# Attention on one core: one ring of three PSUM banks per unit, three banks for pieces, values one slot later

## The chip, the cores and the metric

One core of a Trainium2 chip runs the whole program. TensorE (PE) does matmuls and transposes, VectorE (DVE) and ScalarE (ACT) read its results out of PSUM, GpSimd (POOL) works on SBUF only, SyncE (SP) issues the DMAs. The metric is the device time of one execution in microseconds, lower is better. PSUM has 8 banks of 128 partitions x 512 float32; the program divides them by hand.

## The reference, cut to what matters

Four layers, each as x = x + layernorm(layer(layernorm(x))): a Mamba2 mixer with an MLP, a LoRA MLP, attention, and a linear layer whose weights come from a table. The change touches the third and the fourth, which run interleaved:

```python
def _L1_attn_ref(x, w_qkv, w_o):          # x: 8 batches x 256 tokens x 512
    qkv = x @ w_qkv                        # 32 query heads, 8 key and value heads, 16 wide
    xq, xk = _apply_rope(xq), _apply_rope(xk)
    scores = jnp.einsum('bhsd,bhtd->bhst', xq, keys) * scale
    scores = jnp.where(causal, scores, -jnp.inf)
    probs = jax.nn.softmax(scores, axis=-1)
    out = jnp.einsum('bhst,bhtd->bhsd', probs, values)
    return out @ w_o
```

The kernel keeps float32 accuracy by splitting each operand in a rounded high part and a low part (the difference), and multiplies three times.

## The kernel before, in words

The attention of a batch is cut into 24 **units** (`UNITS`, L1659): for each of the 8 key heads, unit r=0 holds the first 128 queries of its four query heads (they see 128 keys only), and units r=1 and r=2 the last 128 queries of two heads each (256 keys). A unit passes through these steps, each a function of that name:

- `scores(u)` on PE: the products of queries and keys, and one matmul that adds the mask, into a PSUM bank of `S` (two banks, u % 2).
- `maximum(u)` on DVE: the row maxima, negated. `exponentials(u)` on ACT: four or two activations into `p` in SBUF.
- `transposes(u)` on PE: four transposes of `p` into a PSUM bank of `T` (two banks, u % 2).
- `high(u)` on ACT and then `low(u)` on DVE: the turned probabilities as a high and a low part in SBUF (`pT_hi`, `pT_lo`, two buffers each).
- `values(u)` on PE: the product with the values, accumulated over a group of units in the banks `OT`; `values_out` on ACT copies them out.

Beside the units run **pieces** of other work (`JOBS_AT`, L1665, for each of the 24 slots of a batch; `AHEAD`, L1693, for the first batch). On PE a piece is either four transposes (`x`, `a`, `h`: a normalised tile; `q`, `k`: a stack of two-part queries or keys; `back`: attention output) or a half of a projection, six matmuls of 512 columns (`qq`, `o`, `l`), or the whole of `kv`, twelve of 256. Pieces write to the two PSUM banks `X` in turn. `bank_read` makes PE wait, before a piece, until the piece that had the bank before has been read out. Pieces of batch b+1 (its queries and keys) and b-1 (its output projection and the fourth layer) run while the units of batch b do.

The program is a sequence of **slots**. No scheduler works at run time: each engine goes through the slots in its own instruction order, and waits on semaphores. In slot s:

- PE (L2331): `scores(s+1)`, `values(s-2)`, the pieces of slot s, `transposes(s)`.
- ACT (L2056): `drain(s)` (reads out the pieces of slot s-1 that are its own: `x`, `a`, `h`, `q`, `k`, `kv`, `o`), `values_out` in some slots, `high(s-1)`, `exponentials(s+1)`.
- DVE (L2162): `drain(s)` (its own pieces of slot s-1: the rotations after `qq` and `kv`, `back`, `o`, `l`), `maximum(s+1)`, `turned_low(s)` (the low part of a turned tile), `low(s-1)`, then statistics and normalisations of some slots.
- POOL builds the stacks two slots ahead, and does roots and sums.

The waits that matter: `scores(u)` waits for `ex` of unit u-2 (L2209); `transposes(u)` for `ex` of its own unit and `pl` (`low`) of unit u-2 (L2232, L2233); `values(u)` for `pl` of its own unit (L2244). In the text that follows P(n) is the moment at which PE reaches slot n of a batch, that is, at which it issues `scores(n+1)`; n runs from 0 to 23.

Of the kernel before, what the change touches and what calls it, by code (L numbers as in the profile page):

```python
# [1094 lines left out]
def mlps(nc, d, consts, stream, x1_store, w4_store, hT, w0, late, late_2, raw, prod, a_split, lora_unit, bias, tok, old,  # L1095
# [446 lines left out]
    def tensor_program(pe, mixer_program, attention):  # L1542
# [89 lines left out]
        for g, i, j in spots():  # L1632
# [72 lines left out]
def job_tables():  # L1705


    by_slot, ended_by_slot, bank, before, done, turn, stacked, back = {}, {}, {}, {}, {}, {}, {}, {}
    last = [None, None]
    for s in range(FIRST_SLOT, END_SLOT):  # L1710
        by_slot[s], ended_by_slot[s] = [], []
        mine = [(what, part, tile, s // UNITS + rel) for what, part, tile, rel in JOBS_AT[s % UNITS]] if s >= 0 else []
        for what, part, tile, batch in (*AHEAD.get(s, ()), *mine):
            if not 0 <= batch < BATCH:
                continue
            job = name_of(what, part, tile, batch)
            by_slot[s].append((what, part, tile, batch))
            if job not in bank:
                bank[job] = len(bank) % 2
                before[job], last[bank[job]] = last[bank[job]], job  # L1720
            if what not in HALVED or part:
                done[job] = len(done) + 1
                ended_by_slot[s].append((what, part, tile, batch))
                if what in ("x", "a", "h"):
                    turn[what, tile, batch] = len(turn)
                elif what in ("q", "k"):
                    stacked[job] = len(stacked) + 1
                elif what == "back":
                    back[part, tile, batch] = len(back)
    return by_slot, ended_by_slot, bank, before, done, turn, stacked, back  # L1730
# [26 lines left out]
def attention_layer(nc, d, consts, stream, w_hi, w_lo, l_hi, l_lo, bias, keep, xf, yl, small, buffers, ps, mlp):  # L1757
# [223 lines left out]
    def scalar_program(act):  # L1981
# [58 lines left out]
        def high(u):  # L2040
            act.wait_ge(tr, u + 1)
            wait(act, pv, u - 1)
            act.activation(pT_hi[:, u % 2, :], ps[:, T + u % 2, :], ACT.Copy).then_inc(ph, 1)  # L2043

        def exponentials(u):
            act.wait_ge(mx, u + 1)
            wait(act, tr, u - 1)
            heads, width = (4, P) if u % 3 == 0 else (2, SEQ)
            for h in range(heads):
                last = act.activation(p[:, u % 2, h * width:(h + 1) * width],  # L2050
                                      ps[:, S + u % 2, h * width:(h + 1) * width], ACT.Exp, bias=nmax[:, u % 3, h:h + 1])
            last.then_inc(ex, 1)
# [3 lines left out]
        for s in range(FIRST_SLOT, END_SLOT):  # L2056
            b, n = s // UNITS, s % UNITS
            drain(s)
            if n in (0, 2) and in_batch(b - 1):
                values_out(2, n // 2, b - 1)  # L2060
            if n in (9, 11) and in_batch(b):
                values_out(0, n // 2 - 4, b)
            if n in (18, 20) and in_batch(b):
                values_out(1, n // 2 - 9, b)
            if 0 <= s - 1 < SLOTS:
                high(s - 1)
            if 0 <= s + 1 < SLOTS:
                exponentials(s + 1)

    def vector_program(dve, last_sums, end_stats, scale_sum):  # L2070
# [72 lines left out]
        def maximum(u):  # L2143
            heads = 4 if u % 3 == 0 else 2
            dve.wait_ge(sc, u + 1)
            wait(dve, ex, u - 2)
            dve.tensor_reduce(nmax[:, u % 3, 0:heads], ps[:, S + u % 2, :].rearrange("p (h t) -> p h t", h=heads),  # L2147
                              AX, ALU.max, negate=True).then_inc(mx, 1)

        def low(u):  # L2150
            dve.wait_ge(ph, u + 1)
            wait(dve, pv, u - 1)
            dve.tensor_tensor(pT_lo[:, u % 2, :], ps[:, T + u % 2, :], f(pT_hi[:, u % 2, :]), ALU.subtract).then_inc(pl, 1)  # L2153

# [51 lines left out]
    def tensor_program(pe, first, end):  # L2206
        def scores(u):
            b, g, r = u // UNITS, u % UNITS // 3, u % 3
            wait(pe, ex, u - 1)  # L2209
            if u == 0:  # L2210
                pe.wait_ge(setup, 13)
            if u % UNITS == 0:
                pe.wait_ge(st_out, max(STACKED["q", 0, 1, b], STACKED["k", 0, 1, b]))
            elif u % 6 == 0:
                pe.wait_ge(st_out, STACKED["q", g // 2, 1, b])
                if g == 4:
                    pe.wait_ge(st_out, STACKED["k", 1, 1, b])
            bank = ps[:, S + u % 2, :]
            if r == 0:
# [11 lines left out]
        def transposes(u):  # L2231
            pe.wait_ge(ex, u + 1)  # L2232
            wait(pe, pl, u - 1)  # L2233
            if u == 0:
                pe.wait_ge(mlp["summed"], TPB * NG * NB)
            for k in range(4):
                mm = pe.transpose(ps[:, T + u % 2, k * P:(k + 1) * P], p[:, u % 2, k * P:(k + 1) * P], ident)  # L2237
            mm.then_inc(tr, 1)

        def values(u):  # L2240
# [10 lines left out]
            if r == 0:  # L2251
                pe.matmul(ps[:, OT, :], v(0), pT_hi[:, u % 2, :], start=fresh, stop=False)
                mm = pe.matmul(ps[:, OT, :], v(0), pT_lo[:, u % 2, :], start=False, stop=final)
            else:
                out = ps[:, OT + 1, (r - 1) * SEQ:r * SEQ].rearrange("p (h n) -> p h n", h=2)
                of = lambda part, t: part[:, u % 2, :].rearrange("p (h t n) -> p h t n", h=2, t=2)[:, :, t, :]
                for t in range(2):
# [66 lines left out]
        if first == FIRST_SLOT:  # L2324
            pe.wait_ge(mlp["prodd"], unit_at(*LAST_SPOT))
        elif end < END_SLOT:
            pe.wait_ge(mlp["silu"], unit_at(*LAST_SPOT) + 1)
        else:
            pe.wait_ge(masks, 2)
            pe.wait_ge(mlp["w_done"], len(PIECES))  # L2330
        for s in range(first, end):  # L2331
            if 0 <= s + 1 < SLOTS:
                scores(s + 1)
            if 0 <= s - 2 < SLOTS:
                values(s - 2)
            for what, part, t, b in JOBS[s]:
# [391 lines left out]
def later_stages(nc, d, consts, stream, x1_store, w4_store, lut, square, where, ps, mix):  # L2728
# [205 lines left out]
```

## Time and profile before

| | before |
|---|---|
| median of 3 runs | 1779.31 us (1777.43 to 1783.02) |
| the profiled execution | 1781.89 us, span 1780.1 us |
| PE busy | 1654.3 us, 93% |
| weight loads (PEld) | 1378.8 us, 77% |
| DVE busy | 1084.2 us, 61% |
| ACT busy | 803.0 us, 45% |
| POOL busy | 608.7 us, 34% |
| units of attention run | about 1187 to 1730 us |
| one batch of them (24 slots), 1457.7 to 1528.8 us | 71.1 us: PE busy 64.64, DVE 52.39, ACT 51.13 us |

The first 1187 us are the mixer and the two MLPs, which the change leaves alone. The units of the attention layer fill the next 543 us, and 50 us of a tail with the last projections follow. PE's busy time counts a matmul until its modelled end, which overlaps the next one, so the distance between the starts of two matmuls is what one costs. The granted clock of PE is 1.00 of full speed in every batch but the first, and falls only in the tail.

### The profile page before, as it was taken

To read this page: it belongs to the slowest core of one execution; us is meant where nothing else is said; L and a number is where in the kernel's file an instruction comes from. 1 tells how busy PE (TensorE), PEld (TensorE's weight loads), DVE (VectorE), ACT (ScalarE), POOL (GpSimd) and SP (SyncE) were. 2 spreads that over 40 slices of the span, in tenths; PEclk is the share of its full clock that TensorE was granted. 3 is DMA by queue.
4 is the path that set the end of the run, shared out by engine and by line. 5 is a ranking of instruction groups with operands and counts; after the bars stand their busy time and mean duration, and the time that the engine had idled before them with its cause. 6 is when DMAs were issued, how large, how long until landed. Compare 5 with 4: busy or idle time off the path is not lost. (4 is left out here: it accounts for less than half of the span.)

```text
span 1780.1 us, 26343 instructions
## 1 busy us (share of the span) xinstructions
PE 1654.3 (93%) x8965; PEld 1378.8 (77%) x8965; DVE 1084.2 (61%) x2298; ACT 803.0 (45%) x1723; POOL 608.7 (34%) x792
## 2 busy tenths in 40 slices
PE   5999999999999999999999999979988989989884
PEld 4898987888888888777877887867877877778773
DVE  7788886525566554665243324656776776777772
ACT  4676763222332222222122222148777677777760
POOL 5455553211111112341111113474344354344322
PEclk9999999999999999999999999989999999999996
DMA  3000011000111111321011112100000000000000
GB/s 126 30 25 13 5 39 46 24 24 22 30 38 30 35 29 40 110 86 43 19 31 39 28 35 70 55 24 13 1 13 1 13 13 1 13 1 13 13 7 19
DMA packets 32968, 54.27 MB, mean 30 GB/s; under 512 B 3840, under 2 KB 9120, under 8 KB 32832
## 3 DMA queue, kind: packets, MB, share of 16 engines
q1 hardware_dynamic: 32832, 52.55, 9.7%
q8 instruction: 74, 1.21, 0.3%
q14 instruction: 62, 0.51, 0.1%
HBM read 43.10 MB, written 9.44 MB: 30 GB/s over the span
## 5 line engine op out<-in xcount | busy, mean ns | idle before, releaser
L1266 POOL TENSOR_TENSOR m_a_lo<-m_prod,m_a_hi 128x512 fp32r<-128x512 f32 x100 | 134.5, 1345 | 636.4 <-ACT m_a_hi L1348 636.4
L1342 ACT ACTIVATE m_prod<-a_ps 128x512 f32<-128x512 f32 x100 | 59.9, 599 | 543.3 <-PE a_ps L128 543.2
L1501 DVE TENSOR_TENSOR m_prod<-m_prod,a_ps 128x512 f32<-128x512 f32 x100 | 68.8, 688 | 383.8 <-ACT m_prod L1342 383.8
L2050 ACT ACTIVATE t_p<-a_ps,t_nmax 128x128 f32<-128x128 f32 (+1 forms) x512 | 181.7, 426 | 71.3 <-DVE t_nmax L2147 70.6
L2147 DVE TENSOR_REDUCE t_nmax<-a_ps 128x2 f32<-128x512 f32 (+1 forms) x192 | 132.0, 688 | 74.6 <-PE a_ps L2228 40.5
L2153 DVE TENSOR_TENSOR t_pT_lo<-a_ps,t_pT_hi 128x512 fp32r<-128x512 f32 x192 | 131.3, 684 | 39.0 <-ACT t_pT_hi L2043 38.3
L2043 ACT ACTIVATE t_pT_hi<-a_ps 128x512 fp32r<-128x512 f32 x192 | 116.7, 608 | 53.7 <-PE a_ps L2237 53.2
L128 PE MATMUL a_ps<-m_hT_hi,m_w_lo 128*128 128x512 f32 x312 | 124.0, 397 | 0.0
L126 PE MATMUL a_ps<-m_hT_hi,m_w_hi 128*128 128x512 f32 x312 | 123.1, 395 | 0.5 <-DVE f_w_lo L1406 0.5
L127 PE MATMUL a_ps<-m_hT_lo,m_w_hi 128*128 128x512 f32 x312 | 123.3, 395 | 0.0
L2237 PE MATMUL a_ps<-consts,t_p 128*128 128x128 f32 x768 | 115.4, 273 | 0.0
L126 PE MATMUL a_ps<-m_hT_hi,q_w 128*128 128x512 f32 x288 | 113.6, 395 | 1.5 <-DVE m_hT_lo L1406 1.5
L128 PE MATMUL a_ps<-m_hT_hi,q_w 128*128 128x512 f32 x288 | 113.9, 395 | 0.0
L127 PE MATMUL a_ps<-m_hT_lo,q_w 128*128 128x512 f32 x288 | 113.8, 395 | 0.0
L2237 PEld LDWEIGHTS a_ps<-consts,t_p 128*128 128x128 f32 x768 | 92.2, 141 | 9.3
L1348 ACT ACTIVATE m_a_hi<-m_prod 128x512 fp32r<-128x512 f32 x100 | 63.3, 633 | 78.4 <-DVE m_prod L1501 78.4
L1418 DVE TENSOR_TENSOR stream<-a_ps,stream 128x512 f32<-128x512 f32 x128 | 79.5, 683 | 28.2 <-PE a_ps L128 28.2
L126 PE MATMUL a_ps<-f_w_hi,a_w_hi 128*128 128x256 f32 x320 | 93.6, 293 | 2.4 <-DVE a_w_lo L572 2.4
L127 PE MATMUL a_ps<-f_w_lo,a_w_hi 128*128 128x256 f32 x320 | 91.3, 285 | 0.0
L128 PE MATMUL a_ps<-f_w_hi,a_w_lo 128*128 128x256 f32 x320 | 91.2, 285 | 0.0
L2258 PE MATMUL a_ps<-t_pT_hi,t_v 128*128 128x256 f32 x256 | 70.5, 298 | 14.9 <-DVE t_pT_lo L2153 14.3
L126 PE MATMUL a_ps<-m_w_hi,m_a_hi 128*128 128x512 f32 x208 | 83.7, 402 | 0.0
(287 smaller groups left out, 4699.6 us busy)
## 6 DMA issues: line engine op xcount, KB each, us to landing
m_raw<-in_w_mlp SPq DMA_DIRECT2D x75, 256.0 KB, 2.7
a_xt<-in_x SPq DMA_DIRECT2D x8, 512.0 KB, 3.8
t_yl<-in_x SPq DMA_DIRECT2D x16, 256.0 KB, 4.2
x_store<-stream SPq DMA_DIRECT2D x4, 1024.0 KB, 5.2
t_yl<-x_store SPq DMA_DIRECT2D x16, 256.0 KB, 2.7
out<-t_yl SPq DMA_DIRECT2D x16, 256.0 KB, 2.0
m_raw<-in_w_attn SPq DMA_DIRECT2D x10, 256.0 KB, 2.8
a_att<-in_w_mixer SPq DMA_DIRECT2D x8, 256.0 KB, 2.8
```

The lines of the kernel that those rows point to most:

```text
L126: pe.matmul(out, w_hi, x_hi, start=first, stop=False)
L127: pe.matmul(out, w_hi, x_lo, start=False, stop=False)
L128: return pe.matmul(out, w_lo, x_hi, start=False, stop=last)
L1266: pool.tensor_tensor(a_lo[:, n % 2, :], prod[:, :], f(a_hi[:, n % 2, :]), ALU.subtract).then_inc(lo, 1)
L1418: dve.tensor_tensor(tile(i, c), ps[:, ACC + c, :], tile(i, c), ALU.add).then_inc(summed, 1)
L1501: dve.tensor_tensor(prod[:, :], prod[:, :], ps[:, U + TURN_AT["unit", n, 0] % 2, :], ALU.mult).then_inc(prodd, 1)
L2043: act.activation(pT_hi[:, u % 2, :], ps[:, T + u % 2, :], ACT.Copy).then_inc(ph, 1)
L2050: last = act.activation(p[:, u % 2, h * width:(h + 1) * width], ps[:, S + u % 2, h * width:(h + 1) * width], ACT.Exp, bias=nmax[:, u % 3, ...
L2147: dve.tensor_reduce(nmax[:, u % 3, 0:heads], ps[:, S + u % 2, :].rearrange("p (h t) -> p h t", h=heads), AX, ALU.max, negate=True).then_in ...
L2153: dve.tensor_tensor(pT_lo[:, u % 2, :], ps[:, T + u % 2, :], f(pT_hi[:, u % 2, :]), ALU.subtract).then_inc(pl, 1)
L2237: mm = pe.transpose(ps[:, T + u % 2, k * P:(k + 1) * P], p[:, u % 2, k * P:(k + 1) * P], ident)
L2258: pe.matmul(out, v(t), of(pT_hi, t), start=fresh and t == 0, stop=False)
```

## The change

PSUM is divided anew: three banks for pieces (`PIECE_BANKS`) where there were two, and three for units (`UNIT_BANKS`) where there were two for scores and two for turned probabilities. A unit now has one bank for both: its transposes overwrite its own scores. So `scores(u)` waits until `low(u-3)` has read the bank (`pl`), where it waited for `ex` before, and `transposes(u)` waits for its own exponentials alone. `pT_hi` and `pT_lo` get three buffers each (`PT_RING`). PE's order in slot s becomes `scores(s+1)`, `values(s-3)`, `transposes(s)`, pieces. ACT does `high(s-1)` ahead of `values_out`. Two waits at the seam with the MLP move with the banks: the sums of the MLP are awaited by `scores(1)`, and the middle piece of the PE program no longer waits for its `silu`.

```diff
+PIECE_BANKS, UNIT_BANKS = 3, 3
+
+PT_RING = 3
...
-    last = [None, None]
+    last = [None] * PIECE_BANKS
...
-                bank[job] = len(bank) % 2
+                bank[job] = len(bank) % PIECE_BANKS
...
-    X, S, T, OT = 0, 2, 4, 6
+    OT = 6
     last_k = TURN_AT["unit", unit_at(*LAST_SPOT), 0] % 2
+    piece_banks, unit_banks = (1 - last_k, 3 - last_k, last_k), (2 + last_k, 4, 5)
...
         def high(u):
             act.wait_ge(tr, u + 1)
-            wait(act, pv, u - 1)
-            act.activation(pT_hi[:, u % 2, :], ps[:, T + u % 2, :], ACT.Copy).then_inc(ph, 1)
+            wait(act, pv, u + 1 - PT_RING)
+            act.activation(pT_hi[u % PT_RING][:, :], unit_bank(u), ACT.Copy).then_inc(ph, 1)
...
             drain(s)
+            if 0 <= s - 1 < SLOTS:
+                high(s - 1)
             if n in (0, 2) and in_batch(b - 1):
                 values_out(2, n // 2, b - 1)
...
-            if 0 <= s - 1 < SLOTS:
-                high(s - 1)
...
         def scores(u):
             b, g, r = u // UNITS, u % UNITS // 3, u % 3
-            wait(pe, ex, u - 1)
+            wait(pe, pl, u + 1 - UNIT_BANKS)
             if u == 0:
                 pe.wait_ge(setup, 13)
+            if u == 1:
+                pe.wait_ge(mlp["summed"], TPB * NG * NB)
...
         def transposes(u):
             pe.wait_ge(ex, u + 1)
-            wait(pe, pl, u - 1)
-            if u == 0:
-                pe.wait_ge(mlp["summed"], TPB * NG * NB)
             for k in range(4):
-                mm = pe.transpose(ps[:, T + u % 2, k * P:(k + 1) * P], p[:, u % 2, k * P:(k + 1) * P], ident)
+                mm = pe.transpose(unit_bank(u)[:, k * P:(k + 1) * P], p[:, u % 2, k * P:(k + 1) * P], ident)
             mm.then_inc(tr, 1)
...
         if first == FIRST_SLOT:
             pe.wait_ge(mlp["prodd"], unit_at(*LAST_SPOT))
-        elif end < END_SLOT:
+        elif end == END_SLOT:
             pe.wait_ge(mlp["silu"], unit_at(*LAST_SPOT) + 1)
-        else:
             pe.wait_ge(masks, 2)
             pe.wait_ge(mlp["w_done"], len(PIECES))
         for s in range(first, end):
             if 0 <= s + 1 < SLOTS:
                 scores(s + 1)
-            if 0 <= s - 2 < SLOTS:
-                values(s - 2)
+            if 0 <= s - PT_RING < SLOTS:
+                values(s - PT_RING)
+            if 0 <= s < SLOTS:
+                transposes(s)
             for what, part, t, b in JOBS[s]:
...
-            if 0 <= s < SLOTS:
-                transposes(s)
```

## Rows read from the trace of the kernel before

**Rows 1.** Whom PE waited for, 1187 to 1730 us: line, releaser, total, times, longest.
```profile
PE a_ps L2258 <- DVE t_pT_lo L2153: 13.4, 31, 1.4
PE a_ps L126 <- DVE t_hT_lo L2139: 11.1, 18, 0.9
PE a_ps L2304 <- ACT t_kT L2003: 8.2, 12, 0.7
...
PE a_ps L2291 <- DVE t_hT_lo L2139: 3.3, 7, 0.5
...
PE a_ps L2252 <- DVE t_pT_lo L2153: 1.6, 2, 1.0
...
PE a_ps L2291 <- ACT t_kT L2003: 1.3, 6, 0.4
```
**Rows 2.** Timeline of PE, one batch apart: scores in slot 21.
```profile
1450.34 0.48 PE L2226 MATMUL a_ps<-t_kT,t_qT 128*128 128x512 f32 x1
...
1521.45 0.48 PE L2226 MATMUL a_ps<-t_kT,t_qT 128*128 128x512 f32 x1
```
**Rows 3.** Timeline of PE, slot 13: scores, values, then after the piece the transposes.
```profile
1497.92 0.48 PE L2226 MATMUL a_ps<-t_kT,t_qT 128*128 128x512 f32 x1
...
1498.35 0.28 PE L2258 MATMUL a_ps<-t_pT_hi,t_v 128*128 128x256 f32 x1
...
1498.71 0.28 PE L2259 MATMUL a_ps<-t_pT_lo,t_v 128*128 128x256 f32 x1
1500.23 0.60 PE L2237 MATMUL a_ps<-consts,t_p 128*128 128x128 f32 x4
1500.58 0.48 PE L2221 MATMUL a_ps<-t_kT,t_qT 128*128 128x256 f32 x2
```
**Rows 4.** Timeline of DVE: slot 13, then low(14).
```profile
1498.56 0.69 DVE L2147 TENSOR_REDUCE t_nmax<-a_ps 128x2 f32<-128x512 f32 x1 [1.19 <-PE a_ps L2228]
1499.16 0.68 DVE L2153 TENSOR_TENSOR t_pT_lo<-a_ps,t_pT_hi 128x512 fp32r<-128x512 f32 x1
...
1505.73 0.69 DVE L2153 TENSOR_TENSOR t_pT_lo<-a_ps,t_pT_hi 128x512 fp32r<-128x512 f32 x1 [1.58 <-ACT t_pT_hi L2043]
```
**Rows 5.** Timeline of ACT, slots 13 to 15.
```profile
1499.28 0.84 ACT L2050 ACTIVATE t_p<-a_ps,t_nmax 128x256 f32<-128x256 f32 x2 [0.48 <-DVE t_nmax L2147]
...
1503.40 1.19 ACT L2003 ACTIVATE t_kT<-a_ps 64x512 fp32r<-64x512 f32 x2
1504.61 0.60 ACT L1996 ACTIVATE t_qT<-a_ps 128x512 fp32r<-128x512 f32 x1
1505.11 0.59 ACT L2043 ACTIVATE t_pT_hi<-a_ps 128x512 fp32r<-128x512 f32 x1
```
**Rows 6.** Timeline of PE, slots 15 and 16.
```profile
1504.64 0.66 PE L2304 MATMUL a_ps<-consts,t_stacks 128*128 128x128 f32 x4 [0.75 <-ACT t_kT L2003]
...
1505.49 0.48 PE L2226 MATMUL a_ps<-t_kT,t_qT 128*128 128x512 f32 x1
...
1506.48 0.38 PE L2258 MATMUL a_ps<-t_pT_hi,t_v 128*128 128x256 f32 x1 [0.40 <-DVE t_pT_lo L2153]
1506.70 0.28 PE L2259 MATMUL a_ps<-t_pT_lo,t_v 128*128 128x256 f32 x1
```
**Rows 7.** Timeline of DVE, slots 22 to 2 (first and last row) and slot 5.
```profile
1453.28 0.69 DVE L2116 TENSOR_TENSOR t_yl<-a_ps,f_bias 128x512 f32<-128x512 f32 x1 [0.47 <-PE a_ps L128]
...
1466.13 0.68 DVE L2153 TENSOR_TENSOR t_pT_lo<-a_ps,t_pT_hi 128x512 fp32r<-128x512 f32 x1
...
1472.12 0.76 DVE L2083 TENSOR_TENSOR t_rot<-a_ps,consts 128x256 f32<-128x256 f32 x2
...
1473.47 0.69 DVE L2147 TENSOR_REDUCE t_nmax<-a_ps 128x4 f32<-128x512 f32 x1
```
**Rows 8.** Timeline of PE, last batch, slots 7 and 8 (no piece in 7).
```profile
1685.87 0.48 PE L2226 MATMUL a_ps<-t_kT,t_qT 128*128 128x512 f32 x1
...
1687.82 0.38 PE L2258 MATMUL a_ps<-t_pT_hi,t_v 128*128 128x256 f32 x1 [1.35 <-DVE t_pT_lo L2153]
```

More of the change, by code:

```diff
@@ L1800, in bank_of, with unit_bank @@
     def bank_of(job):
-        return ps[:, X + (BANK_OF[job] + 1 - last_k) % 2, :]
+        return ps[:, piece_banks[BANK_OF[job]], :]
+    def unit_bank(u):
+        return ps[:, unit_banks[u % UNIT_BANKS], :]
     def of_heads(ap):
@@ L2050, in exponentials @@
                 last = act.activation(p[:, u % 2, h * width:(h + 1) * width],
-                                      ps[:, S + u % 2, h * width:(h + 1) * width], ACT.Exp, bias=nmax[:, u % 3, h:h + 1])
+                                      unit_bank(u)[:, h * width:(h + 1) * width], ACT.Exp, bias=nmax[:, u % 3, h:h + 1])
             last.then_inc(ex, 1)
@@ L2146, in maximum @@
             wait(dve, ex, u - 2)
-            dve.tensor_reduce(nmax[:, u % 3, 0:heads], ps[:, S + u % 2, :].rearrange("p (h t) -> p h t", h=heads),
+            dve.tensor_reduce(nmax[:, u % 3, 0:heads], unit_bank(u).rearrange("p (h t) -> p h t", h=heads),
                               AX, ALU.max, negate=True).then_inc(mx, 1)
@@ L2151, in low @@
             dve.wait_ge(ph, u + 1)
-            wait(dve, pv, u - 1)
-            dve.tensor_tensor(pT_lo[:, u % 2, :], ps[:, T + u % 2, :], f(pT_hi[:, u % 2, :]), ALU.subtract).then_inc(pl, 1)
+            wait(dve, pv, u + 1 - PT_RING)
+            dve.tensor_tensor(pT_lo[u % PT_RING][:, :], unit_bank(u), f(pT_hi[u % PT_RING][:, :]), ALU.subtract).then_inc(pl, 1)
         def scale(t, b, k, y, before, done):
@@ L2217, in scores @@
                     pe.wait_ge(st_out, STACKED["k", 1, 1, b])
-            bank = ps[:, S + u % 2, :]
+            bank = unit_bank(u)
             if r == 0:
@@ L2251, in values @@
             if r == 0:
-                pe.matmul(ps[:, OT, :], v(0), pT_hi[:, u % 2, :], start=fresh, stop=False)
-                mm = pe.matmul(ps[:, OT, :], v(0), pT_lo[:, u % 2, :], start=False, stop=final)
+                pe.matmul(ps[:, OT, :], v(0), pT_hi[u % PT_RING][:, :], start=fresh, stop=False)
+                mm = pe.matmul(ps[:, OT, :], v(0), pT_lo[u % PT_RING][:, :], start=False, stop=final)
             else:
                 out = ps[:, OT + 1, (r - 1) * SEQ:r * SEQ].rearrange("p (h n) -> p h n", h=2)
-                of = lambda part, t: part[:, u % 2, :].rearrange("p (h t n) -> p h t n", h=2, t=2)[:, :, t, :]
+                of = lambda part, t: part[u % PT_RING][:, :].rearrange("p (h t n) -> p h t n", h=2, t=2)[:, :, t, :]
                 for t in range(2):
@@ L2775, in later_stages @@
     p = over_hi.sb("t_p", [P, 2, 512])
-    pT_hi = over_hi.sb("t_pT_hi", [P, 2, 512], F32R)
+    pT_hi = [over_hi.sb("t_pT_hi", [P, 512], F32R) for _ in range(2)]
+    pT_hi.append(at("t_pT_hi", [P, 512], F32R, of["a_w_hi"] + 13 * KB2))
     oT_0 = over_hi.sb("t_oT", [P, 512])
@@ L2783, in later_stages @@
     qk = [over_raw.sb("t_qk", [P, QK]) for _ in range(2)]
-    pT_lo = at("t_pT_lo", [P, 2, 512], F32R, of["a_cT_hi"])
+    pT_lo = [at("t_pT_lo", [P, 512], F32R, offset) for offset in (of["a_cT_hi"], of["a_cT_hi"] + KB2, of["a_xb"])]
     ao = at("t_ao", [P, 2, DIM], F32, of["a_cT_lo"])
```

## The prediction

> **What bounds the kernel now.** I read the list of waits of PE first, then the timelines of PE, ACT and DVE side by side for one batch, slot by slot. In the units' stretch PE is nearly always at work, and its idle time falls into few kinds [rows 1]. Waits for a bank of the pieces: a projection behind a turned tile's low part (`t_hT_lo`, 11.1 us), a stack behind the eviction of an earlier stack (`t_kT`, 8.2 us), a turned tile behind either (3.3 and 1.3 us), together 23.9 us. Waits of `values` for `low`: 13.4 + 1.6 = 15.0 us. A batch takes 71.11 us from one slot 21 to the next [rows 2]. What PE needs with no wait comes from slot 13 [rows 3]: scores 1498.35 - 1497.92 = 0.43 us (0.55 for r=0), values 1498.71 + 0.12 - 1498.35 = 0.48, half a projection 1500.23 - 1498.83 = 1.40, transposes 1500.58 - 1500.23 = 0.35; four transposes of a piece take 0.44. With 24 units at 1.26 or 1.38 us, 24 small pieces and 14 of 1.40 that is 31.2 + 10.6 + 19.6 = 61.4 us, so 9.7 us a batch are stalls, counted from issue to issue. More banks can win no more than these.
>
> **The links of the new ring.** From the issue of scores to the start of `maximum` 0.64 us [rows 3, 4] (0.76 for r=0), from there to `low` 0.60 [rows 4], from `low` to the matmul that waited for it 1506.48 - 1505.73 = 0.75 [rows 4, 6], from `high` to `low` 0.62 [rows 4, 5], from `maximum` to the exponentials 0.72 [rows 4, 5]. ACT needs 1.21 us for a `k` stack and 0.50 for a `q` stack before it gets to `high` [rows 5]. A stalled matmul is followed by the next after 0.22 us where 0.12 is usual [rows 6], so I add 0.09 for each stall.
>
> **The change part by part.**
> (a) *Third bank for pieces.* It frees every wait of the first kind: `kv` no longer follows the tile `x` before it, `o` and `l` no longer follow `a` and `h`, stacks no longer follow the `k` stack. Worth at most the 23.9 us [rows 1]. In slots 10 and 20 (`o`, `l`) PE's own work follows for several slots, ACT and DVE have slack, and the gain stays: 0.73 us each. In slots 1, 6, 15, 17 and 19 the evictions that PE waited for stand in ACT's and DVE's order ahead of `high` and `low` of the same slot, so there the wait for `low` is next.
> (b) *Scores wait for `low`.* `scores(s+1)` needs `low(s-2)`. Before, the first to need `low(s-2)` was `values(s-2)`, right behind these scores. The deadline comes 0.43 us sooner. The waits of [rows 1] on `t_pT_lo` don't go: they move from `values` to `scores`, though values go a slot later. `ex`, for which scores waited before, shows nowhere in [rows 1] and gives nothing back.
> (c) *Transposes ahead of the pieces.* The pieces come 0.36 us later in the slot. What ACT and DVE drain first in the next slot is these pieces. So a chain piece, drain, `high` or `maximum`, `low`, `scores` has 0.43 + 0.36 = 0.79 us less room than before. Only chains that pass no drain gain room: the transposes are one piece earlier. Transposes now need the exponentials sooner, but in each light slot worked through below scores have waited already, and 0.2 us or more remain: I price this at nothing (the cover is the wait of the scores for `low`); if that cover were gone, each slot behind a rotation (two a batch) would cost up to the 1.35 us of the rotation (1473.47 - 1472.12, [rows 7]).
> (d) *Ring of three units.* A slot can't be shorter than scores, `maximum`, `low`, scores: 0.64 + 0.60 + 0.75 + 0.09 = 2.08 us, 2.20 for r=0. Before, `values` closed the ring behind the scores, 0.43 later: about 1.6 us. Slots with no or one small piece (1.26 or 1.70 us of PE) fall under the new bound.
> (e) *`high` before `values_out`, three `pT` buffers.* Nothing in [rows 1] waits for `pv`; the swap saves up to 0.5 us for one `low` in six slots of a batch, and it is in the sum below. DMAs are not touched.
>
> **The sum, one batch in the middle.** I went through the slots with these links, each engine in its order.
> Slots 13 to 20: 17.6 us of work. Stalls at scores: 0.52 in slot 15 (behind `y_read` and statistics of `o`), 1.66 in slot 16 (ACT evicts a `k` and a `q` stack, then `high(14)`: the chain of [rows 5] unchanged), 0.41 in 17, 1.25 in 18 (the same pair of stacks), 0.67 in 19, 0.44 in 20; 0.18 for the normalised tile in slot 18; 6 x 0.09. Sum 23.3 us. Before: 1521.45 - 1497.92 = 23.53 [rows 2, 3]. The change gives 0.2: ACT and DVE set the pace here and their order is the same.
> Slots 21 to 12: 43.7 us of work. DVE works without a gap from 1453.28 to `low(25)` at 1466.13 [rows 7], 12.85 us that the change can't shorten, and then the whole slot 3 follows where before its scores had been issued: stalls 1.29, 0.44 and 0.89 in slots 1, 2, 3. Slot 6 stalls 0.20. In slot 7 `low(29)` comes behind the rotation, an `x` tile and a `k` stack, 5.16 us after P(5), and scores 0.75 later: stall 0.70, where before the wait of `kv` took 0.90. Slot 10: none. With 5 x 0.09 this is 47.7 us. Before: 1497.92 - 1450.34 = 47.58 [rows 2, 3]. So a batch comes out at 71.0 against 71.1 us: the banks' gain (slots 10 and 20, 1.5 us) is eaten by the earlier deadline (slots 1 to 3, 0.9) and by the stalls that return as waits for `low`. Over six batches: -1 us.
>
> **Last and first batch.** In the last, no pieces of a next batch run; slots 6, 7 and 14 to 17 have none. Before, slot 7 took up to its values 1687.82 - 1685.87 = 1.95 us [rows 8], and empty slots go down to 1.4. By bound (d) and the same stepping, slots 0 to 10 lose 1.7 net and 14 to 20 lose 1.0, with the 0.09s 3.4 us. In the first batch slots 10 to 13 and 20 to 24 hold one small piece or none: 2.08 to 2.20 against 1.6 to 1.9 each, +4.3, less 2.1 for the banks in slots 4 to 6: +2.2. At its start `transposes(0)` wait for the first exponentials with two stacks behind them that covered that wait before: +1. The tail has no units; its chain (turned tile, projection, statistics) has two pieces in flight at most and stays.
>
> **Total**: -1 + 3.4 + 2.2 + 1 = 5.6. Of the 1 us at the start a part falls into gaps that the first slots have anyway, so I take 5. The profiled execution would go from 1781.9 to 1786.9; it lies 2.6 us over the median, so on the median 1779.3 + 5 = 1784.
>
> **A rule that speaks otherwise.** PE shows the same gaps in every batch [rows 1]: 12 times `t_kT`, 18 times `t_hT_lo`. The Trainium skill, *Perfetto Trace Analysis*, section Optimization Strategy, reads consistent bubbles on the engine that should be saturated as possibly too few buffers in SBUF or PSUM. By that, the third bank wins its bubbles. Rival 1 is this case.
>
> **Rivals.**
> 1. *The bank waits go and stay gone.* For: they are 23.9 of PE's waits, and ACT and DVE are idle a quarter of the batch. Against: in five of seven places the releaser is the very eviction that `low` stands behind. All of them gone: 1779 - 24 = 1755; half: 1767. Chance 0.20 for more than 5 us gained.
> 2. *The earlier deadline costs its full 0.79 us wherever a `low` was already late.* These are 33 places [rows 1]: 33 x 0.79 = 26 us, less the 0.73 us in two slots of six or seven batches, 10 us: +16, 1795. It decides if the stalls of slots 1 to 3 and 15 to 20 add up instead of merging, that is if DVE reaches `maximum` late in each. Against: after a stall PE brings work that lets ACT and DVE catch up. Chance 0.36 for more than 5 us lost, of which my own sum lies near the edge.
> 3. *The order does nothing*: the two effects cancel everywhere and the first and last batches too: 1779. This and my forecast share the middle, 0.44.
>
> **Numbers.** A measurement of this kernel can tell about 0.3%, 5.3 us, from no change. Faster 0.20, same 0.44, slower 0.36. The range goes from 1767 (half of rival 1) to 1797 (rival 2 and the start).
>
> **What would show it.** In the profile after: no waits of L126 for `t_hT_lo` and of the stacks for `t_kT` in the middle batches; in their place waits of the scores (L2226, L2221, now on `t_pT_lo`) of 3 to 7 us a batch, in slots 1 to 3, 7 and 15 to 20; `values` never waiting; the transposes of units hardly; a batch of 70.5 to 71.5 us; the last batch 3 us longer. The prediction is wrong if the scores wait less than 2 us a batch (then rival 1), or if the transposes wait for `t_p` in many slots (slower than 1795).

## The result, and the profile after

| | before | after |
|---|---|---|
| median of the runs | 1779.16 us (1776.21 to 1783.02, 8 runs) | 1784.55 us (1782.72 to 1788.82, 8 runs) |
| ratio after to before | | 1.003, 95% interval 1.0018 to 1.0042 |
| the profiled execution, its span | 1781.89, 1780.1 us | 1782.72, 1781.0 us |
| PE, DVE, ACT, POOL busy in the span | 1654.3, 1084.2, 803.0, 608.7 us | 1652.4, 1083.0, 799.6, 607.1 us |
| first to last scores of the units | 1185.68 to 1724.61 | 1181.89 to 1726.10 |

The kernel is 5.4 us slower; 1784.0 had been predicted. The two profiled executions lie only 0.8 us apart because the layers that the change leaves alone took 3.8 us less in the one of after (first scores 1181.89 against 1185.68). From the first scores to the last it is 538.9 against 544.2 us, so the profile shows 5.3 us too, all of it in the stretch that the change touches.

The list of PE's waits, 1187 to 1731 us, of after answers to [rows 1]. Its columns: who waits, for whom, us in total, times, longest. It is the whole list:

```profile
PE a_ps L2236 <- DVE t_pT_lo L2161: 44.1, 56, 1.5
PE a_ps L2231 <- DVE t_pT_lo L2161: 8.8, 25, 1.1
```

L2231 and L2236 are the scores. All waits for a bank of the pieces are gone, values never wait, and one wait has taken the place of all: scores for `low` of three units before. To compare the two lists one needs the whole of both. [rows 1] leaves out five kinds of the list of before, pieces that waited for their own input or for other banks:

```profile
PE a_ps L2291 <- DVE t_xf L1853: 5.5, 7, 0.8
PE a_ps L2304 <- POOL t_stacks L1900: 2.0, 5, 0.4
PE a_ps L2304 <- DVE t_qk L2086: 1.4, 1, 1.4
PE a_ps L2304 <- DVE t_hT_lo L2139: 0.9, 1, 0.9
PE a_ps L2304 <- ACT t_qT L1996: 0.3, 1, 0.3
```

With them the list of before is 38.9 + 10.1 = 49.0 us, and that of after 52.9. PE's idle time in that window went from 51.4 to 53.7 us (544 less the busy time that the windows view gives, 492.64 and 490.27). So nearly all of the idle time stands in the lists, before and after. Eleven kinds of wait became two, and the sum hardly moved.

One batch, slots 15 and 16, timeline of PE, then of DVE, then of ACT in after (start, us, engine and line, what, idle before it and its releaser), against [rows 5, 6]:

```profile
1502.19 0.50 PE L2236 MATMUL a_ps<-t_kT,t_qT 128*128 128x512 f32 x1 [0.35 <-DVE t_pT_lo L2161]
...
1503.56 0.60 PE L2311 MATMUL a_ps<-consts,t_stacks 128*128 128x128 f32 x4
1505.67 0.50 PE L2236 MATMUL a_ps<-t_kT,t_qT 128*128 128x512 f32 x1 [1.51 <-DVE t_pT_lo L2161]
```
```profile
1504.93 0.69 DVE L2161 TENSOR_TENSOR t_pT_lo<-a_ps,t_pT_hi 128x512 fp32r<-128x512 f32 x1 [1.38 <-ACT t_pT_hi L2051]
```
```profile
1502.59 1.19 ACT L2011 ACTIVATE t_kT<-a_ps 64x512 fp32r<-64x512 f32 x2
1503.81 0.60 ACT L2004 ACTIVATE t_qT<-a_ps 128x512 fp32r<-128x512 f32 x1
1504.31 0.59 ACT L2051 ACTIVATE t_pT_hi<-a_ps 128x512 fp32r<-128x512 f32 x1
```

The stack of slot 15 (L2311) no longer waits for the `k` stack of the slot before it (0.75 us in [rows 6]). But ACT's order, `k` stack, `q` stack, `high`, is that of [rows 5]; `low` follows `high` by 0.62, the scores follow `low` by 0.74, and they wait 1.51 us. The bank wait came back as the next wait of the same chain.

Stretches of the unit part, from the issues of scores (us; the first batch begins at its slot 0, with the second scores; the middle is the six batches from slot 0 of batch 1 to slot 0 of batch 7):

| | first batch, from its slot 0 | six middle | batch 4 | last batch |
|---|---|---|---|---|
| before | 58.82 | 426.73 | 71.11 | 52.39 |
| after | 63.42 | 424.03 | 70.97 | 55.77 |

### The profile page after: what moved, and what is told of

The parts are those of the page before. It is cut to its first block and busy times, and to the rows that moved or that the text cites. A ratio compares the mean times of both kernels' runs of the same rounds, so it can differ in the third digit from the quotient of the medians.

```text
span 1781.0 us, 26149 instructions
## 1 busy us (share of the span) xinstructions
PE 1652.4 (93%) x8965; PEld 1383.9 (78%) x8965; DVE 1083.0 (61%) x2298; ACT 799.6 (45%) x1723; POOL 607.1 (34%) x792
## 5 line engine op out<-in xcount | busy, mean ns | idle before, releaser
L2244 PE MATMUL a_ps<-consts,t_p 128*128 128x128 f32 x768 | 115.6, 273 | 1.3 <-ACT t_p L2058 1.3
L2236 PE MATMUL a_ps<-t_kT,t_qT 128*128 128x512 f32 x128 | 60.4, 472 | 44.5 <-DVE t_pT_lo L2161 44.1
L2244 PEld LDWEIGHTS a_ps<-consts,t_p 128*128 128x128 f32 x768 | 91.3, 140 | 10.5 <-ACT t_p L2058 2.2
```

Source lines behind the costliest of these rows:

```text
L2244: mm = pe.transpose(unit_bank(u)[:, k * P:(k + 1) * P], p[:, u % 2, k * P:(k + 1) * P], ident)
```

## The experiments

The table gathers eleven kernels; its last three columns are the stretches above, read from each kernel's own trace. The ratio is to the runs of before made beside the kernel (median 1779.24 us beside e1 to e4, 1779.60 beside b1, b2, e6 and e7, 1778.36 beside e8, e9 and e10), so it is the better measure between them. Its interval is some 2 to 3 us to either side, and a difference of two kernels is known no better.

| kernel | median us | ratio to before (95%) | first | six middle | last |
|---|---|---|---|---|---|
| b1 before, scores wait for low | 1792.72 | 1.0067 (1.0050 to 1.0083) | 65.60 | 431.29 | 56.46 |
| b2 before, transposes ahead of pieces | 1775.81 | 0.9977 (0.9963 to 0.9990) | 60.48 | 421.38 | 52.26 |
| e1 after, two piece banks | 1792.61 | 1.0076 (1.0060 to 1.0092) | 65.16 | 428.59 | 57.29 |
| e2 after, pieces ahead of transposes | 1776.27 | 0.9984 (0.9972 to 0.9995) | 61.69 | 417.67 | 55.27 |
| e3 after, values ahead of scores | 1776.20 | 0.9985 (0.9974 to 0.9997) | 62.62 | 417.46 | 56.16 |
| e6 after, both of these | 1779.73 | 0.9999 (0.9988 to 1.0010) | 61.53 | 421.73 | 54.75 |
| e8 as e6, but scores first in slots 17 to 19 | 1771.92 | 0.9963 (0.9951 to 0.9975) | 61.68 | 416.14 | 54.58 |
| e9 after, high behind values_out | 1794.50 | 1.0092 (1.0074 to 1.0109) | 65.32 | 428.70 | 59.34 |
| e4 four banks for units, two for pieces | 1770.21 | 0.9959 (0.9944 to 0.9974) | 59.32 | 419.20 | 51.38 |
| e7 as e4, pieces ahead of transposes | 1779.16 | 0.9997 (0.9982 to 1.0012) | 59.63 | 425.58 | 51.75 |
| e10 as e4, pieces ahead in slots 1, 16, 18 only | 1777.53 | 1.0003 (0.9989 to 1.0018) | 59.39 | 424.83 | 51.45 |

### The parts of the change, one at a time

The wait alone, added to the kernel before:

```diff
             wait(pe, ex, u - 1)
+            wait(pe, pl, u - 2)
```

> The kernel before with one more wait and nothing else: scores(u) also wait for low(u-3), as in the changed kernel. Theory A (the deadline 0.43 us sooner costs by itself): the waits for t_pT_lo move from the values to the scores; once or twice in each light stretch 0.4 us more, a batch about 72.0 us instead of 71.1; slots with no piece go from 1.4 up to 2.0 us, last batch 2.5 us and first 2.5 us longer: 10 us in all, 1789 us. Rival B (values waited for the same low right behind, so the wait only changes its name): 1779 us.

It costs more than foreseen: 0.67% of 1779 is 12 us. In batch 4 slot 0 goes from 1.70 to 2.75 us, slot 15 from 2.66 to 3.48; slots 1 and 18 give back 0.46 and 0.70. This is the price of the wait that the shared bank brings, paid with the two piece banks still in place.

The third piece bank, taken away from the kernel after:

```diff
-PIECE_BANKS, UNIT_BANKS = 3, 3
+PIECE_BANKS, UNIT_BANKS = 2, 3
...
-    piece_banks, unit_banks = (1 - last_k, 3 - last_k, last_k), (2 + last_k, 4, 5)
+    piece_banks, unit_banks = (1 - last_k, 3 - last_k), (2 + last_k, 4, 5)
```

> The changed kernel with two banks for pieces again (one PSUM bank lies unused), everything else as changed. Theory A (the bank waits are real gain in the slots where PE's own work follows, 10 and 20, and hidden elsewhere): waits for t_hT_lo return, 0.7 us in each of slots 10 and 20, a batch takes 1.5 us more (72.0 us), 10 us in all: 1794 us. Rival B (ACT and DVE alone set the pace of a batch, the banks are worth nothing): a batch stays at 70.5 us and the time within 2 us of 1784.

1792.6: the third bank is worth 8.1 us. In batch 4 only slots 10 and 20 show it (3.65 against 3.17 in after, 3.62 against 3.32); the other slots are equal within 0.05. Those are the two slots that the prediction named, but they are worth 0.8 us a batch and not the 1.5 expected. In the first batch slots 4 to 6 show it (5.12, 2.26 and 3.88 against 3.45, 2.45 and 3.52: 1.8 us). The list of waits of this kernel has only 4.2 us of projections behind `t_hT_lo`, 0.5 at most, where [rows 1] has 11.1:

```profile
PE a_ps L2236 <- DVE t_pT_lo L2161: 37.8, 49, 1.5
PE a_ps L2231 <- DVE t_pT_lo L2161: 6.8, 17, 1.1
PE a_ps L126 <- DVE t_hT_lo L2147: 4.2, 12, 0.5
```

So 12 us for the wait of the shared bank less 8 for the third one leave 4 of the 5.4 us. What came with them (transposes ahead, `high` ahead of `values_out`, values a slot later with a third `pT` buffer) is left with little in sum. Of the trace's 7.8 us (first 1.7, middle 4.6, last 1.5) 1.2 in the last batch is one slot in which the clock fell (below). That the moves of the transposes and of `high` are not nothing one by one is what the next runs show; no run takes back the later values alone, so their share stays open, and the parts need not add up.

The transposes behind the pieces again, in the kernel after:

```diff
             if 0 <= s - PT_RING < SLOTS:
                 values(s - PT_RING)
-            if 0 <= s < SLOTS:
-                transposes(s)
             for what, part, t, b in JOBS[s]:
...
+            if 0 <= s < SLOTS:
+                transposes(s)
```

> The changed kernel with the transposes of a unit at the end of the slot again, behind the pieces. Theory A (the pieces are 0.36 us later in the slot, and the chains through their evictions end so much later): once in each of three stretches of a batch (slots 13 to 20, 22 to 3, 5 to 7) 0.36 us less, a batch 1.1 us shorter (69.5), the wait of the first transposes for the first exponentials gone (1.3 us), 8 to 10 us in all: 1775 us. Rival B (ACT's and DVE's own work sets the pace): no change, 1784. Rival C (early transposes are what lets ACT and DVE get ahead): a batch 1 us longer or more, over 1790 us.

The same move the other way, in the kernel before (transposes ahead of the pieces, all else as it was):

> The kernel before with transposes(s) ahead of the pieces and nothing else, in the old banks. Theory A (evictions of pieces come 0.36 us later against the slots' deadlines): a batch 1.0 us longer (72.1), the first transposes wait 1.3 us for the first exponentials, 7 to 9 us in all: 1787 us. Rival B (early transposes help high and low): under 1779 us.

The first is 8.3 us faster than after, as expected; the second was expected slower and is 3.4 us *faster* than before. (By the ratio it is 4.1. In its trace the six middle batches win 5.4 us, and the first batch loses 1.7 in its slot 0, where the transposes wait for the first exponentials.) The same edit has both signs. The timeline of PE says why. In the kernel with b2's edit, slot 6 of batch 4:

```profile
1472.44 0.60 PE L2237 MATMUL a_ps<-consts,t_p 128*128 128x128 f32 x4
1473.53 0.39 PE L126 MATMUL a_ps<-q_w,t_hT_hi 128*128 128x256 f32 x1 [0.49 <-DVE t_hT_lo L2139]
```

and the same slot of the kernel before:

```profile
1475.75 0.28 PE L2259 MATMUL a_ps<-t_pT_lo,t_v 128*128 128x256 f32 x1
1476.94 0.39 PE L126 MATMUL a_ps<-q_w,t_hT_hi 128*128 128x256 f32 x1 [0.90 <-DVE t_hT_lo L2139]
...
1478.45 0.60 PE L2237 MATMUL a_ps<-consts,t_p 128*128 128x128 f32 x4
```

Before, PE stood 0.90 us at `kv` with four ready transposes behind it; moved ahead they fill 0.41 of that, and the slot goes from 3.85 to 3.52 us. In the kernel after PE never waits at a piece, it waits at the scores, and there the pieces are wanted early, since ACT and DVE drain them ahead of the `low` that frees the bank: with the pieces ahead again (e2), slots 0, 5, 6 and 14 of batch 4 are 0.14, 0.19, 0.16 and 0.35 us shorter.

### Ready work ahead of the wait

If this is the rule, values ahead of the scores fill the scores' wait:

```diff
         for s in range(first, end):
-            if 0 <= s + 1 < SLOTS:
-                scores(s + 1)
             if 0 <= s - PT_RING < SLOTS:
                 values(s - PT_RING)
+            if 0 <= s + 1 < SLOTS:
+                scores(s + 1)
```

> The changed kernel with values(s-3) ahead of scores(s+1) in a slot, the rest as changed. Theory A (scores stand first in the slot and nothing fills their wait for low): values, 0.48 us, never wait and fill part of each stall; once in each of three stretches of a batch 0.3 to 0.48 us less, a batch about 69.4 us, 8 to 10 us in all: 1775 us; empty slots stay at 2.0 us since that ring has no values in it. Rival B: the scores come 0.48 us later, so maximum does, and nothing is gained: 1784.

1776.20: it wins 8.3 us. Both orders together (values, scores, pieces, transposes):

> The changed kernel with both orders: values, scores, pieces, transposes. Theory A: the two gains (0.35 and 0.47 us in slot 14, and once each in slots 0 and 6) act on the same stalls, of which 0.5 us is there in slot 14, so they don't add up: a batch 69.6 us where each alone gave 69.9, plus the 1.3 us at the start: 1773 us, between 1771 and 1775. Rival B (they are independent): a batch 68.9 us, 1768 us or less.

A miss: 1779.73, slower than either alone. The six middle batches of its trace are 69.94, 69.48, 70.60, 69.81, 70.78 and 71.12 us, where those of e2 are 68.96, 69.59, 69.61, 69.92, 69.60 and 69.99: two are a little shorter (the second and the fourth), four about 1 us longer. The windows view of one core, 1438 to 1446 us, in the third of them (window, its length, PE busy, granted clock, DMA share, GB/s) shows another cause:

```profile
1438.00:1440.00 2.00, 0.89 (x5) 0.35 (x3) 1.15 (x2) 2.00 (x7) 0.00 (x0) 1.00 0.00 0
1440.00:1442.00 2.00, 1.07 (x10) 0.90 (x9) 1.80 (x5) 1.68 (x5) 1.17 (x3) 0.96 0.00 0
1442.00:1444.00 2.00, 2.00 (x10) 1.90 (x10) 0.70 (x3) 1.43 (x4) 1.55 (x3) 0.50 0.04 8
1444.00:1446.00 2.00, 2.00 (x14) 2.00 (x13) 2.00 (x5) 1.29 (x3) 0.00 (x0) 0.68 0.00 0
```

Here the columns behind the length are PE, weight loads, DVE, ACT and POOL, then the clock. Two waits came close together, both in slot 18 (I took them for slots 17 and 18 when I wrote the next expectation), and PE's clock fell from 2.4 to 1.2 GHz behind them:

```profile
1439.59 0.50 PE L2236 MATMUL a_ps<-t_kT,t_qT 128*128 128x512 f32 x1 [1.11 <-DVE t_pT_lo L2161]
...
1441.14 0.63 PE L2298 MATMUL a_ps<-consts,t_xf 128*128 128x128 f32 x4 [0.93 <-DVE t_xf L1861]
```

The windows in steps of 2 us show such a fall four times in the middle of this kernel, at 1302, 1442, 1582 and 1654 us, one in each of the batches 1, 3, 5 and 6, the long ones. To test that this is the loss, scores go ahead of the values in slots 17 to 19 alone; the values then stand between the two waits, and the second has less to wait (the edit is against the kernel of e6):

```diff
         for s in range(first, end):
+            if s % UNITS in (17, 18, 19) and 0 <= s + 1 < SLOTS:
+                scores(s + 1)
             if 0 <= s - PT_RING < SLOTS:
                 values(s - PT_RING)
-            if 0 <= s + 1 < SLOTS:
+            if s % UNITS not in (17, 18, 19) and 0 <= s + 1 < SLOTS:
                 scores(s + 1)
```

> The kernel after with the order values, scores, pieces, transposes, save in slots 17 to 19 of each batch, where scores stand ahead of the values. With that order in all slots the time was 1779.7 us, against 1776.2 with either half of it, and batches 1, 3, 5 and 6 took 1.2 us more than 2 and 4, two of them with PE's granted clock at 0.50 for 2 us and 0.68 for 2 us behind two waits of about 1 us close to each other (slots 17 and 18). Theory A (the clock is what that order lost): the two waits lie apart again, the clock stays at 1.00, all middle batches take 69.5 to 69.9 us, and the time is 1775 (1773 to 1777). Theory B (the two changes of order don't add up because the waits for the low part only move, whatever the clock does): the middle batches keep a sum of 421 to 422 us and the time stays at 1779 to 1780.

1771.92, 1 us below the range of Theory A. The two waits of slot 18 are 1.10 and 0.47 us, and from 1184 us on the clock is over 0.95 in every 2 us of the unit part. Batches 1, 3, 5 and 6 become 1.28, 1.32, 1.46 and 1.30 us shorter, batches 2 and 4, which had no fall, 0.10 and 0.13. So of the 5.6 us that the middle gained some 4.9 are the falls. The mean clock of a whole execution says that it was so in all runs of e6, not only in the profiled one: it is 0.979 to 0.983 in its 12 runs, and 0.985 or 0.986 in 11 of the 12 of e8. Without the falls the two orders together come to about what had been expected of them (1773), in a kernel that has one of them in 21 of 24 slots only.

### Four banks for the units

The shared bank makes a ring of three. With one more bank for the units and one fewer for the pieces:

```diff
-PIECE_BANKS, UNIT_BANKS = 3, 3
+PIECE_BANKS, UNIT_BANKS = 2, 4
...
-    piece_banks, unit_banks = (1 - last_k, 3 - last_k, last_k), (2 + last_k, 4, 5)
+    piece_banks, unit_banks = (1 - last_k, 3 - last_k), (last_k, 2 + last_k, 4, 5)
```

> The eight banks divided otherwise: four for units, two for pieces; orders as changed. Scores wait for low(u-4). Theory A (the ring of three units is what costs the 3.4 us in the last batch, the 4.6 us in the first and slots 1 to 3): waits of scores for low under 1 us a batch; last batch 3 us shorter, first 3 us shorter; in the middle the bank waits of slots 6, 10 and 20 return (0.7 us each) and the later deadline gives 1 to 2 us back, a batch 70 to 71 us; 1776 us, between 1770 and 1782. Rival B: 1784, with the waits at the transposes for t_p instead.

1770.21, better than the 1776 expected and faster than both kernels. The last batch takes 51.38 us, less than before the change (52.39), so the ring was what made it 55.77. The kernel with two piece banks and three unit banks (e1) leaves one bank unused, and differs from this one in nothing but the fourth unit bank: 1792.6 against 1770.2. The same spare bank is worth 22.4 us in the ring of the units and 8.1 in that of the pieces. Scores wait no more, and PE's list begins:

```profile
PE a_ps L2244 <- ACT t_p L2058: 20.5, 37, 1.3
PE a_ps L126 <- DVE t_hT_lo L2147: 5.3, 13, 1.1
PE a_ps L2311 <- ACT t_kT L2011: 4.9, 12, 0.4
PE a_ps L2298 <- DVE t_xf L1861: 4.0, 7, 0.6
```

The transposes (L2244) now wait for the exponentials, 20.5 us, with the pieces behind them. By the rule of ready work the pieces should go ahead:

> Four unit banks, two piece banks, and the pieces ahead of the transposes. Theory A: the 21.8 us that the transposes waited for t_p go, waits for piece banks and evictions take most of their place since ACT's and DVE's order in the light slots is the same, a batch 69.6 us (70.0 with transposes first), the start 1.3 us shorter: 1766 us, between 1763 and 1769. Rival B: all of it turns into waits for banks: 1770 us.

A miss by 13 us: 1779.16, 9 us slower. The rule was too simple. Waits for `t_p` fell to 4.6 us, and those of the stacks for `t_kT` rose from 4.9 to 14.2, of projections from 5.3 to 12.2 and of normalised tiles for `t_xf` from 4.0 to 10.0. That left open whether the order only has to be chosen slot by slot (the edit is against the kernel of e4):

```diff
-            if 0 <= s < SLOTS:
+            if s % UNITS not in (1, 16, 18) and 0 <= s < SLOTS:
                 transposes(s)
             for what, part, t, b in JOBS[s]:
...
+            if s % UNITS in (1, 16, 18) and 0 <= s < SLOTS:
+                transposes(s)
```

> The kernel with four banks for units and two for pieces (1770.2 us), with the pieces ahead of the transposes in slots 1, 16 and 18 alone. There its transposes waited for the exponentials (0.73, 0.35 and 0.67 us in one batch); in slots 2, 6, 10, 15, 17 and 18 it is the pieces that wait for a bank. Theory C (ready work has to stand ahead of whatever waits, slot by slot): the three waits are filled by the pieces, 1 to 1.5 us a batch and 6 to 9 us in all less what comes back as bank waits: 1765 (1762 to 1768). Theory D (the pieces later in the slots are what feeds ACT and DVE in time, and any order but one that is the same in all slots only shifts the wait to the next stack): 1770 (1768 to 1773) or worse.

1777.53: it wins nothing. Slot 1 of an undisturbed batch (6) goes from 3.31 to 3.74, slot 2 from 2.44 to 2.02; slot 18 from 3.36 to 3.79, slot 19 from 2.78 to 2.39: what one slot wins the slot before it has lost. PE in slot 18 of batch 3, first with the transposes ahead of the piece everywhere, then in this kernel, whose execution is 1.36 us later at that point:

```profile
1434.84 0.66 PE L2244 MATMUL a_ps<-consts,t_p 128*128 128x128 f32 x4 [0.67 <-ACT t_p L2058]
...
1436.08 0.63 PE L2298 MATMUL a_ps<-consts,t_xf 128*128 128x128 f32 x4 [0.58 <-DVE t_xf L1861]
```
```profile
1437.45 0.65 PE L2298 MATMUL a_ps<-consts,t_xf 128*128 128x128 f32 x4 [1.91 <-DVE t_xf L1861]
1437.92 1.04 PE L2244 MATMUL a_ps<-consts,t_p 128*128 128x128 f32 x4
```

The piece is a tile that DVE normalises (L1861) behind a `low`, and it is ready at the same moment in both (1437.45 - 1.36 = 1436.09). It was ready *after* the exponentials. Put first, it turned waits of 0.67 and 0.58 us into one of 1.91, with the ready transposes behind it: slot 18 is 0.43 longer. I had picked the slots by the transposes' wait and not asked what stood behind it. The long wait had a second price: the 1.04 us of the transposes is the slower clock, 0.50 at 1438, and such a fall lies in each of the batches 2 to 5, which take 71.00 to 71.44 us where they took 69.69 to 70.04; batches 1 and 6, without one, take 70.10 and 70.07 against 70.01 and 70.06. So the order itself is worth nothing here (the second expectation), and of the loss of 5.6 us in the middle 5.5 are the clock.

### High behind values_out

```diff
             drain(s)
-            if 0 <= s - 1 < SLOTS:
-                high(s - 1)
             if n in (0, 2) and in_batch(b - 1):
...
+            if 0 <= s - 1 < SLOTS:
+                high(s - 1)
             if 0 <= s + 1 < SLOTS:
                 exponentials(s + 1)
```

> The kernel after with ACT's high part behind values_out, as in the kernel before: part (e) of the change undone alone. My prediction gave it up to 0.5 us for one low part in six slots of a batch, in the sum. Theory A: the six slots are 0, 2, 9, 11, 18 and 20; only in 0, 2, 18 and 20 a low part is late there, and ACT's copy of 0.5 us falls on the path of two of them at most, 0.3 to 1 us a batch, 2 to 6 us in all: 1787 (1785 to 1790). Theory B (DVE with its own queue, not ACT, sets when the low part comes in these slots): no change, 1784.5 (1783 to 1786).

1794.5, 10 us slower than after, outside both expectations. The timeline of ACT, then of DVE and PE, in slot 2 of batch 4, in after and then here:

```profile
1463.42 0.60 ACT L1994 ACTIVATE t_hT_hi<-a_ps 128x512 fp32r<-128x512 f32 x1
1463.90 0.61 ACT L2051 ACTIVATE t_pT_hi<-a_ps 128x512 fp32r<-128x512 f32 x1
1464.72 0.60 ACT L2046 ACTIVATE t_oT<-a_ps 128x512 f32<-128x512 f32 x1 [0.21 <-PE a_ps L2266]
...
1465.45 0.68 DVE L2161 TENSOR_TENSOR t_pT_lo<-a_ps,t_pT_hi 128x512 fp32r<-128x512 f32 x1
...
1466.19 0.50 PE L2236 MATMUL a_ps<-t_kT,t_qT 128*128 128x512 f32 x1 [0.63 <-DVE t_pT_lo L2161]
```
```profile
1472.95 0.60 ACT L1994 ACTIVATE t_hT_hi<-a_ps 128x512 fp32r<-128x512 f32 x1
1474.24 0.60 ACT L2046 ACTIVATE t_oT<-a_ps 128x512 f32<-128x512 f32 x1 [0.70 <-PE a_ps L2266]
1474.73 0.59 ACT L2051 ACTIVATE t_pT_hi<-a_ps 128x512 fp32r<-128x512 f32 x1
...
1475.36 0.69 DVE L2161 TENSOR_TENSOR t_pT_lo<-a_ps,t_pT_hi 128x512 fp32r<-128x512 f32 x1 [0.30 <-ACT t_pT_hi L2051]
...
1476.10 0.50 PE L2236 MATMUL a_ps<-t_kT,t_qT 128*128 128x512 f32 x1 [1.02 <-DVE t_pT_lo L2161]
```

`high` starts 0.48 us behind the start of the turned tile's copy (L1994) in the one, 1.78 in the other. Only 0.49 of the difference is the copy of the values; most of the rest is that this copy waits 0.70 us for the *values* of its unit, which the change made a slot later. DVE has other work that hides 0.9 us of that; then `low` waits for `high`, and the scores wait 1.02 us instead of 0.63. Batch 4 is 0.72 us longer (slot 2 by 0.39, slot 18 by 0.33). In slot 0 `high` is late too, by 1.2 us, and DVE's own work hides all of it: the slot takes 3.13 us, 3.14 in after. Over the whole trace ACT stands before the copy of the values 48 times of 48 here, 42.4 us in all; in the kernel before, with the same order on ACT and values a slot earlier, it does so once, 1.6 us. The six middle batches lose 4.7 us, inside the 2 to 6 expected; the first loses 1.9, the last 3.6, the tail behind the units 1.6. Of the last batch's 3.6, 1.24 is slot 8, where the clock fell.

## Why the prediction was right, step by step

**The total.** 1784.0 against 1784.55. The sum was +5, the medians say +5.4 and the trace's unit part +5.3. The result lies at the edge of what the chances called the same (0.3%). The stretches behind the sum:

| | predicted | measured |
|---|---|---|
| batch 4, slots 13 to 20 | 23.3 | 23.30 |
| batch 4, slots 21 to 12 | 47.7 | 47.68 |
| six middle batches | -1 | -2.7 |
| last batch | +3.4 | +3.4 |
| first batch with its start | +3.2 | +4.6 |

Batch 4 was the one stepped through, and it came out to 0.02 us, stall by stall and not by luck: the scores of after wait 1.18, 0.30, 0.63 and 0.55 us in its slots 1, 2, 3 and 7 (predicted 1.29, 0.44, 0.89 and 0.70) and 0.35, 1.51, 0.25, 1.11, 0.48 and 0.19 in slots 15 to 20 (predicted 0.52, 1.66, 0.41, 1.25, 0.67 and 0.44). The prediction counts from issue to issue, the trace from the end of the matmul before, and that accounts for some 0.15 of each difference. Only slot 6, given 0.20, has no wait.

But one batch stood for six: 71.1 less 71.0 was rounded to "-1 for six", where batches 4 and 6 gained 0.14 and 0.10, batches 2, 3 and 5 about 0.45 and batch 1 1.13.

In the first batch slot 0 takes 4.63 us where it took 2.92, 1.7 and not 1: its transposes wait 1.32 us for the exponentials, and then go at the granted clock of 0.50 (0.90 us to the next matmul; in before, later in the slot, 0.57). Slots 4 to 6 save 2.2 (predicted 2.1), the others lose 5.1 (predicted 4.3, for slots 10 to 13 and 20 to 24).

So the first batch was 1.4 us dearer than predicted and the middle 1.7 us cheaper; that these two cancel is luck, and so is a sum that is right to half a microsecond.

**(a) Third bank.** Right in mechanism and place, and here a run shows it: in a middle batch it pays in slots 10 and 20 alone, in the first in slots 4 to 6. I said 0.73 us in each of slots 10 and 20; against before they are 0.66 and 0.63 shorter, of which the bank alone gives 0.48 and 0.30 (e1). The rest fits the transposes moved ahead of the piece: that move alone, in the kernel before, makes them 0.17 and 0.36 shorter (b2). The whole is 8.1 us by the medians.

**(b) and (d) The earlier deadline and the ring of three.** Right. The waits of `values` went to `scores` and values wait nowhere. The wait alone costs 12 to 13 us (b1), and a fourth unit bank takes 22.4 us off the same kernel with three (e1 to e4), 5.9 of the trace's in the last batch (57.29 to 51.38, of which 1.2 is a fall of the clock in e1). The floor of 2.08 to 2.20 us a slot: slots 5 and 8 of the last batch take 2.11 and 2.12, slots 4 and 7 2.00 and 1.99, so the estimate was 0.1 too high. Slot 7 of the last batch goes from 2.88 to 1.99 and slot 6 from 1.33 to 3.00, a wait that changed its slot.

**(c) Transposes ahead.** The direction was right in this kernel only: it costs 8.3 us there (e2). What I wrote, that the pieces come 0.36 us later and the chain loses so much room, holds where PE waits at the scores. It isn't a property of the order: in the kernel before the same move wins 3.4 us (b2), since PE waited at the pieces there. This step failed as a general rule, and I repeated the failure in the expectation of b2.

**The price of nothing.** The transposes' wait for exponentials was put at nothing, with the scores' own wait as cover. In after that holds: PE's timeline has it once, at the start:

```profile
1185.04 1.11 PE L2244 MATMUL a_ps<-consts,t_p 128*128 128x128 f32 x4 [1.32 <-ACT t_p L2058]
```

1.32 us where I had said 1. And when the cover went (e4, where scores don't wait) it came at 20.5 us in 37 places; two slots a batch had been named for that case, and it is more than four.

**(e) High ahead of values_out.** Mis-sized. I had it as up to 0.5 us for one `low` in six slots, and thought of it as a small extra. It carries 10 us (e9). The term that I left out: values a slot later make `values_out` wait for them, so without the swap ACT stands ahead of `high` in every one of the six slots, 42.4 us in all. That [rows 1] shows no wait for `pv` was no argument, since those are PE's waits and it is ACT that waits for `pv`. It did no harm to the sum, since that stepped through ACT in its new order, but a prediction of the change without this line would have been 10 us wrong.

**The rivals.** Rival 1, the bubbles filled and the gain kept: the waits of [rows 1] did go, all 38.9 us and the 10.1 beside them, and 52.9 us of another kind came. The Trainium skill, *Perfetto Trace Analysis*, section Optimization Strategy, reads a gap that repeats as a possible lack of buffers. The runs agree in part: a third bank wins 8.1 us where all else stays (e1), a third of the 23.9 us of gaps behind a bank. What the trace could tell ahead is which of the gaps are whose: a bank behind which PE has its own work, and not a chain through ACT. Rival 2, 0.79 us in 33 places, put 1795; b1 and e1, where no third bank helps, came to 1793, but by a few slots and not by all, as their slot times show.

## What to carry to other kernels

With engines that run in a fixed order, a wait costs what can't run behind it: for every wait that stays, put ahead of the waiting instruction what is ready by then, and check in the trace that it is ready earlier, since the same move of four transposes won 3.4, cost 8.3 and won 9 us in three kernels that differ in which wait stands last. Give a spare buffer to the ring that stands last: one bank was worth 8.1 us to the pieces and 22.4 to the units. Before two buffers are merged into one, step the longest chain through the shared one and compare it with the shortest slot; here four banks for the units and two for the pieces take 1770.2 us where three and three take 1784.6. When a step is moved later, look for the reader behind it on another engine: it waits too, and so does all that is queued behind it.

## What the runs showed of the chip

Before these runs the granted clock seemed no matter in the unit part. It does matter, in kernels that on paper are better. In e6 and e10 it fell from 2.4 to 1.2 GHz (0.50) for 2 to 4 us, four times each, behind stretches of 2 us in which PE was busy 0.89 and 1.07 us (e6) and 0.55 us (e10, 1436 to 1438). One fall costs 1.2 to 1.5 us. PE had waited 1.1 and 0.9 us close together, or 1.9 at once, and was at work again when the clock fell. Where the falls lie is seen in the one profiled execution of each kernel alone; that the others have them too shows in their mean clock, 0.979 to 0.983 in the 12 runs of e6 and 0.975 to 0.982 in the 12 of e10, against 0.984 or 0.985 in five of the six of e4. Single falls lie in the first or last batch of b1, e1, e3, e7 and e9 too, and are in their columns above. The same waits don't always do it. In the last batch of after and of e9, PE rows of the same two slots:

```profile
1686.92 0.50 PE L2236 MATMUL a_ps<-t_kT,t_qT 128*128 128x512 f32 x1 [1.48 <-DVE t_pT_lo L2161]
...
1688.91 0.50 PE L2231 MATMUL a_ps<-t_kT,t_qT 128*128 128x256 f32 x2 [0.47 <-DVE t_pT_lo L2161]
1689.26 0.39 PE L2233 MATMUL a_ps<-t_mask,t_id_r 128*128 128x512 f32 x1
```
```profile
1699.38 0.50 PE L2236 MATMUL a_ps<-t_kT,t_qT 128*128 128x512 f32 x1 [1.47 <-DVE t_pT_lo L2161]
...
1701.38 0.73 PE L2231 MATMUL a_ps<-t_kT,t_qT 128*128 128x256 f32 x2 [0.47 <-DVE t_pT_lo L2161]
1701.90 0.63 PE L2233 MATMUL a_ps<-t_mask,t_id_r 128*128 128x512 f32 x1
```

Equal waits, to 0.01 us, and the clock stays in the first and falls in the second, which makes slot 8 3.36 us instead of 2.12. Why, these traces don't show. A comparison of two orders that differ by a few us should look at the clock in short stretches first: the mean over the span shows four falls only in its third digit (0.981 against 0.986) and not where they are, and the profiled executions of e1, e3 and e9, with one fall each, have 0.981 as well.
